# Cross-attention and sign FFN on one core: FFN weights loaded in square blocks and turned by VectorE

## What is computed

```python
h = layernorm(x)                                    # latents
q = h @ Wq                                          # 32 heads of 128
k, v = concat(ctx, h) @ Wk, concat(ctx, h) @ Wv     # 4 kv heads, 256 keys
x = x + softmax(q @ k.T / sqrt(128)) @ v @ Wo
y = layernorm(x)
routing = softmax(y @ gate_w.T)                     # 8 experts
out = x + (y * (routing @ in_scale)) @ sign(weight).T * (routing @ out_scale) + bias
```

## Time and profile before

| | us |
|---|---|
| median of 3 runs | 661.77 (660.36 to 662.10) |
| profiled execution | 660.18 |
| its span | 658.4 |
| TensorE busy | 650.3 |
| VectorE busy | 483.4 |
| GpSimd busy | 396.3 |
| ACT busy | 376.5 |

### The profile page before, as it was taken

How to read it: one execution, slowest core, us unless ns; L and a number is a source line. 1 busy time by engine, 2 the same in 40 slices (tenths; PEclk the granted TensorE clock), 3 DMA queues, 4 the chain that set the end, 5 groups by cost and what they waited for, 6 DMA issues and landing times.

```text
span 658.4 us, 11059 instructions
## 1 busy us (share of the span) xinstructions
PE 650.3 (99%) x3298; PEld 547.1 (83%) x3298; DVE 483.4 (73%) x915; ACT 376.5 (57%) x925; POOL 396.3 (60%) x315
## 2 busy tenths in 40 slices
PE   8999999999999999999999999999999999999996
PEld 6888888888888888888888888888888888878875
DVE  5652232678897889788878887888788788979866
ACT  4344242675575558555764675557556755676643
POOL 3236665287476458545954595457546759974686
PEclk9999999999999999999999999999999999999999
DMA  9656665477898787788878888887888888776612
GB/s 327 251 204 223 239 248 192 154 264 237 283 294 257 258 271 260 260 263 272 272 241 265 270 288 254 265 277 253 262 264 274 256 284 261 256 261 225 189 67 82
DMA packets 96476, 161.68 MB, mean 246 GB/s; under 512 B 9064, under 2 KB 49256, under 8 KB 95392
## 3 DMA queue, kind: packets, MB, share of 16 engines
q1 hardware_dynamic: 96416, 160.97, 74.8%
HBM read 108.38 MB, written 52.56 MB: 244 GB/s over the span
## 4 chain that ended last, share of the span: by engine, by line
PE 95%; POOL 1%; issue 1%; DVE 1%; ACT 1%; POOLq 0%; DVEq 0%
PE bank L1766 24%; PE bank L1550 23%; PE bank L1692 20%; PE bank L1731 13%; PE bank L1610 6%; PE bank L1846 2%; PE bank L1803 1%; PE bank L1747 1%; POOL wo_pair L668 1%; PE bank L1591 1%; PE bank L1567 1%; PE bank L1795 1%; PE bank L1559 1%; PE bank L1751 0%; PE bank L1818 0%
## 5 line engine op out<-in xcount | busy, mean ns | idle before, releaser
L632 POOL TENSOR_TENSOR p_low<-p_low,p_high 128x1024 fp32r<-128x1024 f32 x64 | 153.7, 2402 | 156.6 <-ACT p_high L774 156.5
L1766 PE MATMUL bank<-wo_pair,oT 128*128 128x512 f32 x720 | 175.9, 392 | 0.3 <-POOL wo_pair L668 0.3
L911 ACT ACTIVATE prob<-bank,nmax 128x256 f32<-128x256 f32 x256 | 119.0, 471 | 70.2 <-DVE nmax L1287 65.1
L1766 PEld LDWEIGHTS bank<-wo_pair,oT 128*128 128x128 f32 x720 | 131.0, 188 | 25.5 <-POOL wo_pair L668 1.0
L1550 PEld LDWEIGHTS bank<-kg,qT 128*128 128x128 f32 x768 | 107.8, 190 | 9.9 <-issue 0.2
L1287 DVE TENSOR_REDUCE nmax<-bank 128x2 f32<-128x512 f32 x128 | 87.2, 684 | 37.9 <-PE bank L1550 37.3
L1550 PE MATMUL bank<-kg,qT 128*128 128x256 f32 x768 | 111.2, 282 | 0.0
L1307 DVE STREAM_TRANSPOSE p_turned<-prob 128x512 f32<-128x512 f32 x128 | 90.0, 704 | 26.0 <-ACT prob L911 21.3
L774 ACT ACTIVATE oT<-bank 128x512 fp32r<-128x512 f32 x64 | 38.3, 598 | 111.8 <-DVE bank L1321 111.8
L1692 PE MATMUL bank<-xT,wq_ring 128*128 128x512 f32 x336 | 82.4, 391 | 0.0
L662 POOL TENSOR_TENSOR wq_ring<-raw_a,wq_ring 128x512 fp32r<-128x512 f32 x42 | 54.4, 1295 | 27.8 <-ACT wq_ring L774 27.8
(11 more groups left out here) (143 smaller groups left out, 936.3 us busy)
## 6 DMA issues: line engine op xcount, KB each, us to landing
p_park<-p_turned SPq DMA_DIRECT2D x64, 512.0 KB, 3.6
p_low<-p_park SPq DMA_DIRECT2D x64, 512.0 KB, 5.8
kg<-k_park SPq DMA_DIRECT2D x64, 256.0 KB, 3.2
vg<-v_park SPq DMA_DIRECT2D x64, 256.0 KB, 3.8
v_park<-v_stage SPq DMA_DIRECT2D x8, 1024.0 KB, 4.4
raw_a<-in_L_xattn_Wq SPq DMA_DIRECT2D x32, 256.0 KB, 5.4
raw_b<-in_L_xattn_Wo SPq DMA_DIRECT2D x32, 256.0 KB, 5.3
k_park<-k_stage SPq DMA_DIRECT2D x8, 1024.0 KB, 4.1
```

Source lines behind the costliest of these rows:

```text
L632: nc.gpsimd.tensor_tensor(part, part.bitcast(fp32), p_high[:, :].rearrange("p i c q -> p (i c q)"), ALU.subtract).then_inc(p_lo, 1)
L911: ins = nc.scalar.activation(prob[:, p, j], s_bank[p][:, j * KEYS:(j + 1) * KEYS], ACT.Exp, bias=nmax[:, p, j:j + 1], accum_out=esum[:, t ...
L1766: last = nc.tensor.matmul(wo_bank[:, :], oT[:, s, h, :], wo_pair[:, w, h, :], start=((s, w) == TERMS[0] and h == 0), stop=((s, w) == TERMS ...
```

## The change

The weights are loaded another way. Chunk c now holds columns 128c to 128c+127 of the matrix, as 16 blocks of 32x32 in each group of 32 partitions: partition 32i + s holds, for j = 0 to 15, the 32 values in row 32j + s, columns 128c + 32i to 128c + 32i + 31. With a 32x32 transpose inside each block the chunk is the transposed matrix. So VectorE makes the turn by one instruction per chunk (`sgn_turn`), from `ffn_raw[c]` into `oscale[:, c]`, and ACT copies from there. The signs on GpSimd are made one step later (steps 52 to 55), the loads are one chunk per step in steps 50 to 53, TensorE's transposes are gone, and on ACT the last two copies stand behind the second `exps` of step 57. The diff, with blank lines left out:

```diff
             def load_ffn(c):
-                sp.dma_start(ffn_raw[c], ffn_w[c * P:(c + 1) * P, :]).then_inc(ffn_in[c], 16)
+                blocks = ffn_w.rearrange("(j s) (c i r) -> c i s j r", s=32, c=HC, r=32)[c]
+                for i in range(QB):
+                    sp.dma_start(ffn_raw[c][32 * i:32 * i + 32].rearrange("s (j r) -> s j r", r=32), blocks[i]
+                                 ).then_inc(ffn_in[c], 16)
...
-                    if last and t == 2:
-                        sp.wait_ge(wq_lo, split(q + 1, 3))
-                        sp.wait_ge(sum_ready, summed(q + 1, 3))
-                        load_ffn(0)
-                        load_ffn(1)
-                    if last and t == 3:
-                        sp.wait_ge(x_ready, T2_READ)
-                        load_ffn(2)
-                        load_ffn(3)
+                    if last and 2 <= t < 2 + HC:
+                        if t == 2:
+                            sp.wait_ge(wq_lo, split(q + 1, 3))
+                            sp.wait_ge(sum_ready, summed(q + 1, 3))
+                        if t == 4:
+                            sp.wait_ge(x_ready, T2_READ)
+                        load_ffn(t - 2)
...
             def sgn(c):
-                pool.wait_ge(ffn_in[c], 16)
+                pool.wait_ge(ffn_in[c], 16 * QB)
...
-                if last and qd == QUADS - 2 and 3 <= t < 3 + HC:
-                    sgn(t - 3)
+                if last and qd == QUADS - 2 and 4 <= t < 4 + HC:
+                    sgn(t - 4)
...
             def sgn_copy(c):
                 act.wait_ge(sgnt_ready, c + 1)
-                copy(sgnT[:, c, :], proj_bank[c % 2][:, :]).then_inc(sgnt_copied, 1)
+                copy(sgnT[:, c, :], oscale[:, c]).then_inc(sgnt_copied, 1)
...
+                if t + LEAD < B:
+                    exps(g, qd, t + LEAD, 1)
                 if t == 1:
                     sgn_copy(2)
                     sgn_copy(3)
-                if t + LEAD < B:
-                    exps(g, qd, t + LEAD, 1)
...
+            def sgn_turn(c):
+                dve.wait_ge(sgn_ready, c + 1)
+                dve.wait_ge(x_ready, 8 * (G * QUADS - 1))
+                dve.wait_ge(z2_ready, 6 * (G * QUADS - 1))
+                nc.vector.transpose(oscale[:, c], ffn_raw[c]).then_inc(sgnt_ready, 1)
...
                 row_recip(*ahead)
                 if not final:
                     accumulate(g, qd, t)
+                else:
+                    sgn_turn(0)
+                    sgn_turn(1)
...
                     row_recip(g, qd, t + LEAD)
+                if t == 1:
+                    sgn_turn(2)
+                    sgn_turn(3)
...
-            def sgn_transpose(c):
-                pe.wait_ge(sgn_ready, HC)
-                if c >= 2:
-                    pe.wait_ge(sgnt_copied, c - 1)
-                else:
-                    pe.wait_ge(proj_lo, count(G - 1, UNITS, QUADS - 1, PRE_UNITS + UNITS))
-                for r in range(HC):
-                    last = nc.tensor.transpose(proj_bank[c % 2][:, r * P:(r + 1) * P],
-                                               ffn_raw[r][:, c * P:(c + 1) * P], ident[:, :])
-                last.then_inc(sgnt_ready, 1)
...
-                if final:
-                    sgn_transpose(0)
-                    sgn_transpose(1)
...
-                if t == 1:
-                    sgn_transpose(2)
-                    sgn_transpose(3)
```

## The result

| | before | after |
|---|---|---|
| median of 5 runs, us | 661.29 (660.36 to 662.10) | 670.29 (668.08 to 671.91) |
| profiled execution, us | 660.18 | 671.03 |
| its span, us | 658.4 | 669.2 |

The ratio is 1.0132, 95% interval [1.0114, 1.0150]: by the ratio 8.7 us slower, where 5.9 were forecast. The direction and the two stalls came as forecast; 2.8 us of the sum were missing.

A forecast was written before the change was run, and what follows sets the result against it. TensorE, 99% busy, bounds the kernel. Of 1.74 us removed 0.6 count; +3.9 by late sgn and +2.7 by late yt_copy make +5.9: 666.1 us profiled, 667.7 with the median 1.6 above; range 664.0 to 671.5.

The forecast's parts named there:

- the two stalls: TensorE waits 3 to 4 us on GpSimd's wo_pair in step 56, and 2.8 us for ACT's yT at logits(0).
- What bounds the kernel: TensorE, busy 99% of the span, with GpSimd near at step 56 and ACT's yT at logits(0).
- Part 1: Sixteen transposes leave TensorE, 1.74 us; the first group gives nothing, 0.6 of the second group's 0.87 us comes back.
- Part 2: Late signs on GpSimd delay wo_rest in step 56 by 4.2 us: +3.9 us, +3.3 after the transposes' gain.
- Part 3: VectorE's turns and ACT's copies ahead of yt_copy(0) delay logits(0), +2.7 us more; +5.96 us there in all.
- E: End of ACT's last two exponentials of step 57, forecast at 594.4; logits(0) were to start at E + 3.54.
- Part 4: Loads in steps 50 to 53: four issues per block at 0.43 us each, at most 2.5 us a block, no delay.
- a wait in steps 52 to 55: Sign of being wrong: TensorE waits in these steps; rival 3 has it waiting for p_high there.
- Rival 4: TensorE's clock falls in one of the new waits, the next 3 us taking twice as long: +3, 670.7 us; 12%.
- Rival 1: One stall only: turns reach ACT early and yt_copy(0) follows unhindered: +3.3, 665.1 us; 10%.
- Rival 2: Faster: the four wo_rest hide behind TensorE's products, only the 1.74 us count: 660.0 us; 4%.
- rival 3: Loads hold p_low by dear packets: some 680 us at the upper price, about 670 at half of it; 9%.

The follow-up runs named there:

- Run 12: Changed kernel, signs in steps 51 to 54, turns and copies in idle places, 16 plain loads of 32 whole rows (weights wrongly arranged): 662.17 us, ratio 1.0006.
- run 2: The turns-early kernel: changed kernel with turns and copies 2 and 3 right behind 0 and 1 in step 56, signs still late: 666.43 us, ratio 1.0091.
- Run 1: Changed kernel with GpSimd's four signs back in steps 51 to 54, as before the change: 666.42 us, ratio 1.0087.
- run 4: Changed kernel with unread products filling TensorE's waits, 12 ahead of project_first in step 56 and 11 ahead of logits(0) in step 58: 668.77 us, ratio 1.0123.
- Run 5: Kernel before with the new square loads alone, signs and TensorE's turns as before (weights wrongly arranged): 663.05 us, ratio 1.0022.
- run 6: Kernel before with four issues per chunk, each loading 32 whole rows of 2 KB: 661.44 us, ratio 1.0001.
- run 7: Kernel before with the square loads alone, each chunk issued right behind the fetch of p_low instead of ahead of it: 666.79 us, ratio 1.0079.
- run 8: Changed kernel with signs in steps 51 to 54, turns and copies in idle places, loads behind the fetch of p_low: 665.73 us, ratio 1.0071.
- run 3: Changed kernel with signs in steps 51 to 54 and all four turns and copies in step 56: 664.19 us, ratio 1.0054.
- run 9: Changed kernel with signs in steps 51 to 54, turns and copies in idle places, square loads ahead of the fetch of p_low: 663.80 us, ratio 1.0035.

## Why the prediction was right, and where its sum fell short

**What bounds the kernel: right.** Each wait put on TensorE came out in the time, and the places named, GpSimd at step 56 and `yT` at `logits(0)`, were those of the two stalls.

**Part 1: right, even generous.** The transposes were to give 0.6 of 1.74 us. Run 12 shows that they give about nothing under the best conditions tried.

**Part 2: right.** `wo_rest` was to start 4.2 us later (measured 4.2, counted from `p_rest` of step 56), TensorE to wait on each head: 2.89 and 0.51 us of idle time between shorter ones. In the turns-early kernel, where a clock fall of 3.4 us is the only other term known in it, the stretch is 11.67 us against 11.4. Run 1 gives 3.0 us back, against 3.3 for the stall: the fall that goes with it gives more, the uncovered turns take some.

**Part 3: right.** `logits(0)` at E + 3.45 (forecast 3.54), wait 2.65 us (2.8), worth 2.7 us in run 2 (forecast 2.66, but the measured figure has the clock fall in it; in run 4, without the fall, the stretch is 9.92 us against 10.1). A turn takes 0.64 us, not 0.70. The sentence that turns 0 and 1 are hidden, and cost at most 1.4 us if the cover goes, was borne out: 0.99 us in run 1.

**Part 4: wrong, the step of the sum that failed.** "I take at most 2.5 us a block and no delay" was an argument about the packets on the 16 engines, and about them the outcome bears it out, though not the working: a line through 82 ns at 1676 B and 54 ns at 1260 B is below nothing at 128 B, so it could not price such a packet. There are 7872 more packets, yet the queue's busy time goes from 74.8% of 658.4 us to 74.0% of 669.2 us, 2.7 us more per engine for the same bytes, or, with 492 more packets for each, some 5 ns for an added packet.

But SP's own issue was costed at 0.43 us each from plain transfers, which gave "2.4 us of slack against 1.0 to 1.7" for step 54. The fetch of step 55, behind the fourth load, got no working of its own. For this fetch the trace shows: `r_park` holds SP 1.5 us longer, the load 2.3 us, so with the 0.84 us by which this execution was late already before the first load it is issued at 562.54 in place of 557.90, 4.6 us later. It lands 5.9 us on, at 568.4, as ACT begins `p_high` (565.91 before). It had some 2.0 us of slack, so 2.5 are left. ACT itself comes to it 0.95 us later than before, so it waits 1.59 us, and TensorE 1.19.

Run 5 prices the part at 1.4 us; run 6 shows that the packets' form does it and not the count of issues. Had I taken what stands behind the loads on SP, with an issue that could be longer, the sum would have had a term for it. The prediction had named a wait in steps 52 to 55 as a sign of being wrong, and for this part it was one.

The Trainium skill, "DMA: Bandwidth & Descriptors" (Measured), was weighed there as speaking against the change. What it says is of transfers under 64 KB, and the issues here are of just 64 KB, so it reaches them only nearly. At that size the runs let the rows decide: 16 transfers with 2 KB rows in run 6 cost nothing, those with 128 B rows in run 5 cost 1.4 us.

**Rival 4, the clock, came true beside the forecast, not in its place.** It was given 12% and 3 us. The clock fell twice, to 0.50, for about 6.8 and 3.4 us. The falls cost 0.95 us behind the first wait, the time for which `p_low` lay ready, and 1.2 us at the scores. Work that fills 6.8 us at half clock takes 3.4 at the full one, so the first fall could have cost 3.4 us; it cost less because the products in it would have waited for GpSimd anyway. The 3 us of work at half clock with which the rival was priced stood in no row; in the traces of all runs the falls lasted 3.4 or 6.8 us. The argument "these waits have work on both sides" was the faulty one: in the kernel before the longest wait of TensorE behind its first stage is 0.3 us, so its rows could not carry that.

**Rivals 1 and 2** are refuted by both waits being there; rival 3 in its kind was true (the loads hold `p_low`), by another resource than it said and at 1.4 us, not 2 to 12.

**The sum against the measurement:** 5.9 forecast; + 1.4 for the loads; + about 2 for the clock; − some tenths for what these overlap gives 9, measured 8.7. That the time stayed in the range is in part luck: its upper end was built from the fall of the clock or from dear packets, not from both, and both came, each small enough for the sum (667.7 + 1.4 + 2 = 671.1) to stay under 671.5. That the two profiled executions differ by 10.8 us is no contradiction: 0.84 of it was there before step 50, with none of the changed code run, and the profiled execution of before is at the fast end of its runs.

## What to carry to other kernels

Work taken off the busiest engine is worth only what its neighbours' slack allows: before moving it, lay the timelines of all the engines it lands on beside it and ask who stands behind it there, the queue that issues the transfers among them. A rearranging load is not free because its bytes are the same; count its packets, and price what the issuing queue has to do next. In these traces a fall of TensorE's clock came with each of the five waits of 2.64 to 2.95 us, on top of the wait and of every other term; with such a wait in the forecast it belongs in the range of each case, not beside them as a case of its own.

## What the runs showed of the hardware that I had not expected

- Short packets hold the queue that issues them. In the kernel after, four issues of 512 packets of 128 B take 2.0 to 2.7 us (1.82 to 1.84 with 2 KB rows in run 6), the next large fetch 0.8 to 1.7 in place of 0.38, and four issues right behind a 512 KB fetch 2.3 to 5.0 (runs 7 and 8). The issue of the fetch was longer, but its landing, counted from the issue's start, was not: 4.3 to 6.7 us for the four fetches behind the loads, against 5.0 to 6.8 before.
- The same packets take little of the transfer engines' time: some 5 ns for each one added, an estimate from two busy shares (74.8% and 74.0%) that are given to a tenth of a per cent.
- TensorE's granted clock went to 0.50 with the waits of 2.89 and 2.65 us in the kernel after, 2.64 in run 1, 2.88 in run 2 and 2.95 in run 7, and stayed there through as much as 6.8 us of nearly unbroken work. In runs 3, 9 and 12, whose waits are 1.6 us or less, it stayed at 1.00 from 578 to 606 us, and also behind the 2.38 us of run 8. In run 4, where products fill the same waits, it stayed at 1.00. The Trainium skill, "TensorE: Matmul & The Clock Gate" (Part 1), has idleness halve the clock, and these traces agree.
